# One home per chunk for the gathered rows of a recommendation tower, one semaphore per gathered slot, and the loops over chunks written out

## The reference

```
e = jnp.stack([tbl_0[ids[:, 0]], ..., tbl_25[ids[:, 25]]], axis=1)   # 512 x 26 x 64
x = layer_norm(dense_t @ Wd.T, gd, bd)                                # 512 x 128
y = layer_norm(jnp.einsum('bnd,ed->bne', e, Ws), gs, bs)              # 512 x 26 x 128
y = jnp.einsum('bne,pn->bep', y, Wsi)
y = jnp.swapaxes(layer_norm(y, gsi, bsi), 1, 2)                       # 512 x 32 x 128
T = jnp.concatenate([x[:, None, :], y], axis=1)
Z = jnp.einsum('bnd,bmd->bnm', T, T)                                  # 33 x 33 per sample
z = layer_norm(Z[:, TRIL_I, TRIL_J] @ Wl.T, gl, bl)                   # 512 x 512, 384 used
h = relu(concatenate([z, dense_t]) @ W_top1 + b_top1)
y = relu(h @ W_top2 + b_top2) @ W_top3
```

## Time and profile before

| what | value |
|---|---|
| time, median of 3 runs | 259.2 us (258.77 to 259.23) |
| profiled execution, span from first to last instruction | 258.3 us |
| PE busy | 183.6 us (71%) |
| DVE, ACT busy | 100.9 us (39%), 90.1 us (35%) |
| POOL busy, x104 gathers of 966 ns mean | 101.3 us (39%) |
| mean granted TensorE clock | 0.822 |

### The profile page before, as it was taken

The page is one execution under the profiler, slowest core; times in us unless marked ns, Lnnn a source line. Parts: engine busy times, 40 slices in busy tenths (PEclk is TensorE's granted clock), DMA queues, the critical chain, the costliest instruction groups (busy, mean ns, idle before and its releaser), DMA issues.

```text
span 258.3 us, 4239 instructions
## 1 busy us (share of the span) xinstructions
PE 183.6 (71%) x1616; PEld 117.3 (45%) x1616; DVE 100.9 (39%) x193; ACT 90.1 (35%) x221; POOL 101.3 (39%) x113
## 2 busy tenths in 40 slices
PE   1696913859295662948487569574849989999996
PEld 1343903516144252625264433443446466649476
DVE  2766003361078270526263401615254288623120
ACT  2442100710073340636034302523235276522333
POOL 4887772777405265445373720727250000000000
PEclk9999555695779595698777959859597999999999
DMA  6423235111100011015210100134110004123000
GB/s 171 150 67 111 56 107 173 28 27 25 20 1 19 15 21 22 10 20 129 41 23 10 33 10 0 22 94 68 21 25 0 0 0 116 27 86 53 3 0 0
DMA packets 19391, 11.67 MB, mean 45 GB/s; under 512 B 14256, under 2 KB 16816, under 8 KB 19376
## 3 DMA queue, kind: packets, MB, share of 16 engines
q1 hardware_dynamic: 16048, 8.05, 11.5%
q0 software_dynamic: 3328, 3.41, 6.9%
HBM read 9.29 MB, written 2.16 MB: 44 GB/s over the span
## 4 chain that ended last, share of the span: by engine, by line
PE 52%; issue 21%; another core or an unknown queue 13%; DVE 8%; ACT 4%; DMA 1%; SPq 0%; ACTq 0%; DVEq 0%
PE proj_ps L482 12%; PE dots_ps L473 8%; PE o_ps L501 6%; PE mix_ps L450 4%; PE quad_ps L461 4%; DVE var_p L786 2%; PE proj_ps L518 2%; PE turn_ps L501 2%; PE turn_ps L442 1%; PE proj_ps L396 1%; PE o_ps L505 1%; PE mix_ps L518 1%; PE o_ps L551 1%; PE dots_ps L551 1%
## 5 line engine op out<-in xcount | busy, mean ns | idle before, releaser
L373 POOL DMA_INDIRECT e_rows<-table_dram,rows_sb x104 | 100.5, 966 | 90.3 <-DVE e_unit L822 59.6
L473 PE MATMUL dots_ps<-feats 128*32 128x33 f32 x1024 | 27.0, 208 | 46.1 <-issue 45.9
L482 PE MATMUL proj_ps<-f_sb,proj_w 128*128 128x512 f32 x64 | 47.2, 878 | 5.7 <-issue 3.2
L473 PEld LDWEIGHTS dots_ps<-feats 128*32 128x32 f32 x1024 | 18.5, 117 | 55.8 <-issue 54.0
L786 DVE TENSOR_REDUCE var_p<-y_sq 128x16 f32<-128x512 f32 x32 | 21.4, 683 | 24.3 <-ACT y_sq L616 21.5
L818 DVE RECIPROCAL rstd_n<-std_n 128x8 f32<-128x8 f32 x16 | 3.2, 201 | 66.3 <-ACT std_n L636 61.5
L450 PE MATMUL mix_ps<-mixw_sb,e_unit 128*128 128x192 f32 (+4 forms) x128 | 21.7, 315 | 10.3 <-DVE e_unit L822 10.3
L616 ACT ACTIVATE y_sq<-proj_ps 128x512 f32<-128x512 f32 x32 | 18.7, 595 | 28.0 <-PE proj_ps L482 14.5
L482 PEld LDWEIGHTS proj_ps<-f_sb,proj_w 128*128 128x128 f32 x64 | 15.4, 266 | 22.8 <-issue 17.1
L450 PEld LDWEIGHTS mix_ps<-mixw_sb,e_unit 128*128 128x128 f32 x128 | 20.4, 201 | 11.0 <-DVE e_unit L822 10.9
L461 PEld LDWEIGHTS quad_ps<-gram,e_cols 128*128 128x128 f32 x104 | 18.5, 244 | 12.2 <-issue 12.1
(11 more groups left out here) (131 smaller groups left out, 179.2 us busy)
## 6 DMA issues: line engine op xcount, KB each, us to landing
z_dram<-z_mine SPq DMA_DIRECT2D x4, 512.0 KB
e_rows<-table_dram,rows_sb POOLq DMA_INDIRECT x104
w_sb<-w_dram SPq DMA_DIRECT2D x2, 512.0 KB, 4.7
wl_sb<-wl_dram SPq DMA_DIRECT2D x2, 512.0 KB
w_sb<-w_dram SPq DMA_DIRECT2D x1, 768.0 KB
z_pairs<-z_dram SPq DMA_DIRECT2D x12, 64.0 KB
dense_sb<-dense_t_dram SPq DMA_DIRECT2D x1, 512.0 KB
wl_sb<-wl_dram SPq DMA_DIRECT2D x1, 256.0 KB
```

The source lines that it names most:

```text
L373: pool.indirect_dma_start(out=e_rows[:, t, D * ab:D * (ab + 1)], out_offset=None, in_=table, in_offset=bass.IndirectOffsetOnAxis(ap=rows_s ...
L473: mm = pe.matmul(dots_ps[PR * k:PR * (k + 1), (PR + 1) * g:(PR + 1) * (g + 1)], f[:, 2:PR + 2], f[:, 0:PR + 1], start=True, stop=True)
L482: pe.matmul(proj_ps[:, ab, :], proj_w[:], f_sb[:, q % 2, ab, :], start=True, stop=True).then_inc(projected, 1)
```

## The change

`e_rows` gets a second index, the chunk, so each gathered row has a place of its own and POOL waits for nothing but the row numbers. There is one semaphore per slot (16 in place of 4), and the waits on it are for 32 times its number of tiles in every chunk. The helper `slots` runs all steps from a Python loop, so nothing is a hardware loop any more on PE, ACT, DVE or SP, and every wait compares with a constant. What is computed, its order on each engine and the sizes of all instructions are the same.

```
-        e_rows = sb("e_rows", [P, TILES, 2 * D])
+        e_rows = sb("e_rows", [P, CHUNKS, TILES, 2 * D])
...
-        gathered = [sem(f"gathered{q}") for q in range(QUARTERS)]
+        gathered = [[sem(f"gathered{chunk}_{q}") for q in range(QUARTERS)] for chunk in range(CHUNKS)]
...
-            peeled = -(-latest // QUARTERS) * QUARTERS
-            for s in range(peeled):
-                slot(s // QUARTERS, s % QUARTERS, s)
-            with eng.Fori(peeled // QUARTERS, CHUNKS) as chunk:
-                for q in range(QUARTERS):
-                    slot(chunk, q)
-            for s in range(SLOTS, SLOTS + latest):
+            for s in range(SLOTS + latest):
                 slot(s // QUARTERS, s % QUARTERS, s)
...
-            return with_last(lambda chunk: None if isinstance(chunk, int) else stage(chunk))
+            return with_last(lambda chunk: stage(chunk) if chunk < CHUNKS - 2 else None)
...
-            sp.wait_ge(gathered[0], 32 * tiles_of(0)[1])
+            sp.wait_ge(gathered[0][0], 32 * tiles_of(0)[1])
...
-            with sp.Fori(1, CHUNKS - 1) as chunk:
+            for chunk in range(1, CHUNKS - 1):
...
-                    wait(pool, unit_ready, QUARTERS * (chunk - 1) + q + 1)
...
-                                out=e_rows[:, t, D * ab:D * (ab + 1)], out_offset=None, in_=table,
+                                out=e_rows[:, chunk, t, D * ab:D * (ab + 1)], out_offset=None, in_=table,
...
-                            ).then_inc(gathered[q], 16)
+                            ).then_inc(gathered[chunk][q], 16)
...
-                pe.wait_ge(gathered[q], chunk * (32 * nt) + 32 * nt)
+                pe.wait_ge(gathered[chunk][q], 32 * nt)
...
-                    mm = pe.transpose(turn_ps[:, P * t:P * (t + 1)], e_rows[:, t0 + t, :], eye_sb)
+                    mm = pe.transpose(turn_ps[:, P * t:P * (t + 1)], e_rows[:, chunk, t0 + t, :], eye_sb)
```

More of the change, by code:

```diff
@@ L260, in tower, with slots, slot @@
         block = ctx.enter_context(nc.Block())
-        def slots(eng, stages, extra=()):
+        def slots(stages, extra=()):
             latest = max(late for late, _ in stages)
-            def slot(chunk, q, s=None):
+            def slot(chunk, q, s):
                 for late, stage in stages:
-                    if s is None or 0 <= s - late < SLOTS:
+                    if 0 <= s - late < SLOTS:
                         stage(chunk + (q - late) // QUARTERS, (q - late) % QUARTERS)
@@ L314, in _ @@
             sp.dma_start(pairs_sb[:], pairs).then_inc(pairs_in, 16)
-            sp.wait_ge(gathered[0], 32 * tiles_of(0)[1])
+            sp.wait_ge(gathered[0][0], 32 * tiles_of(0)[1])
             sp.dma_start(w1_sb[:, 0:KU, :], w1[:, 0:KU, :]).then_inc(w1_in, 16)
             for q in range(1, QUARTERS):
-                sp.wait_ge(gathered[q], 32 * tiles_of(q)[1])
+                sp.wait_ge(gathered[0][q], 32 * tiles_of(q)[1])
                 begin, end = (q - 1) * KZ // 3, q * KZ // 3
@@ L526, in top_1_early @@
                 top_1(0, 0, CHUNKS - 2)
-            slots(pe, [(3, project), (1, quad), (0, turn), (2, mix), (4, dots), (8, in_loop(turn_o)), (7, in_loop(linear))],
+            slots([(3, project), (1, quad), (0, turn), (2, mix), (4, dots), (8, in_loop(turn_o)), (7, in_loop(linear))],
                   extra=[(1, sum_x), (1, top_bl), (3, lambda: weigh_moments(0, 3)),
@@ L708, in save_o @@
                          o_turn_ps[:, 0:USED].rearrange("p (j s b) -> p j s b", s=1, b=P)).then_inc(o_saved, 1)
-            slots(act, [(8, in_loop(square_o)), (2, root_n), (3, square), (3, root_p), (8, in_loop(root_o)),
+            slots([(8, in_loop(square_o)), (2, root_n), (3, square), (3, root_p), (8, in_loop(root_o)),
                         (8, in_loop(scale_o)), (0, save_cols), (3, place_x), (2, save_f), (4, save_z), (8, in_loop(save_o)),
@@ L794, in variance_n @@
                 wait(dve, std_ready, s)
-                dve.wait_ge(gathered[q], chunk * (32 * nt) + 32 * nt)
+                dve.wait_ge(gathered[chunk][q], 32 * nt)
                 dve.tensor_tensor(e_prod[:, 0:2 * nt, :].rearrange("p a d -> p (a d)"), quad_ps[:, 0:P * nt],
-                                  e_rows[:, t0:t0 + nt, :].rearrange("p t d -> p (t d)"), ALU.mult).then_inc(prod_done, 1)
+                                  e_rows[:, chunk, t0:t0 + nt, :].rearrange("p t d -> p (t d)"), ALU.mult).then_inc(prod_done, 1)
                 dve.wait_ge(prod_done, s + 1)
@@ L822, in norm_n @@
                 dve.tensor_tensor(e_unit[:, t0:t0 + nt, :].rearrange("p t (a d) -> p (t a) d", d=D),
-                                  e_rows[:, t0:t0 + nt, :].rearrange("p t (a d) -> p (t a) d", d=D),
+                                  e_rows[:, chunk, t0:t0 + nt, :].rearrange("p t (a d) -> p (t a) d", d=D),
                                   rstd_n[:, 0:2 * nt].unsqueeze(2).to_broadcast([P, 2 * nt, D]),
@@ L867, in invert_o @@
                 dve.reciprocal(o_rstd[:], o_std[:]).then_inc(orstd_done, 1)
-            slots(dve, [(2, norm_n), (8, in_loop(variance_o)), (3, variance_p), (8, in_loop(invert_o)), (3, norm_p),
+            slots([(2, norm_n), (8, in_loop(variance_o)), (3, variance_p), (8, in_loop(invert_o)), (3, norm_p),
                         (1, variance_n)],
```

## The result

| what | before | changed |
|---|---|---|
| time, median of 4 runs | 259.0 us (258.0 to 259.2) | 282.4 us (281.3 to 282.9) |
| profiled span | 258.3 us | 281.1 us |
| PE busy | 183.6 us | 153.1 us |
| mean granted TensorE clock | 0.822 | 0.780 |

The ratio is 1.090, 95% interval 1.086 to 1.095. The change costs 23 us, and 282.4 lies outside the range of the prediction; of its cases "frozen", 275 us, comes nearest.

What follows compares the result with a forecast made beforehand. Gathers on POOL were taken to slow PE's completions. PE free at about 138 us and step 5 at 147 or 141, plus 72.0 and 46.3 us, gave spans of 265.3 and 259.3, forecast 262 us, range 246 to 271.

Steps and rivals of the forecast that it cites:

- frozen: Rival: PE's completions stand still while gathers run, step 5 starts at 156 us, time 275 us; chance 0.13 with nearly frozen.
- The bound: Gathers are almost never late; while they run, PE completes passes at a small rate, so POOL's pauses matter.
- first sign: ACT and DVE show "remote" waits of tens of us before 138 us, the first at L829, past 41.8.
- the release: PE is free 1.4 to 3.6 us after POOL's last gather at 135.7 us, so from about 138 us.
- The second: the rate: Beside gathers without a break PE completes 0.57 to 0.83 passes per us, 64 to 93 passes by 138 us.
- the low rate: 0.57 passes per us: PE at the end of step 3 when freed at 138 us, step 5 starting near 147.
- the high rate: 0.83 passes per us: 93 passes, PE in step 4 when freed at 138 us, step 5 starting at 141.
- the two spans: Predicted profiled spans of 265.3 us at 0.57 passes per us and 259.3 us at 0.83, middle 262.
- The short-batch rate: Rival: PE keeps 1.9 to 2.9 passes per us beside gathers, kernel gets faster, put at 247 us; chance 0.38.
- rival 2: PE keeps the short batches' rate of 1.9 to 2.9 passes per us beside gathers, 247 us; chance 0.38.

Runs made afterwards that it cites:

- set 4 pair: Changed kernel unedited, 282.1 us, and changed kernel with only POOL's 12 waits put back, 256.6 us, on a chip where before took 260.9 us.
- e16_half_rows: Changed kernel with gathers of 64 rows in place of 128, on a chip where before took 260.9 us: 287.9 us.
- e1: Changed kernel with POOL's wait put back, on a chip where before took 194.4 us: 192.1 us, ratio 0.990.
- e9: Changed kernel with POOL's wait put back, on a second chip where before took 194.2 us: 193.1 us, ratio 0.998.
- e15: Changed kernel with a 512-column memset on POOL before each gather, one gather each 1.78 us, where before took 260.9 us: 244.6 us.

## Why the prediction was wrong

**What held.** The bound and the sign of its mechanism: gathers are almost never late on a held chip, they slow PE's completions, and the change takes away the pauses. The set 4 pair puts 25.5 us on POOL's wait, more than the 21.2 us that the change lost in that set, and so nothing on the written-out loops and semaphores, as the prediction had it. Its first sign came true as well: L821, which is L829 of before, started at 71.15, past 41.8. That it got slower was forecast with a chance of 0.52 only. POOL's end, 135.7 predicted, is 136.03. After the release: steps 5 to 15 were to cost 72.0 us and took 73.25 (161.43 to 234.68); the rest from step 16, 46.3 predicted, took 46.4. `dots` of step 4 did come in one burst after the release (158.90), though none of them before it.

**The step that failed: the release.** "With 1.4 to 3.6 us for the release PE is free from about 138 us" took the lag after a batch for a constant. It grows with the batch. The rows had it: after the first 26 gathers the lag was 3.6 us, after 20 also 3.6, after the six of step 5 about 1.4, and I carried the values on as they were. Set against the number of gathers they are 0.14, 0.18 and 0.23 us each, which gives 14 to 24 us for 104; 14.85 were measured, and that the first batch comes so close is luck, since the three disagree. What does agree is the time from the start of a batch to its release: 1.46, 1.42 and 1.42 us per gather (the last from 78.99 to 87.5), and 1.415 in the new one. The step cost 12.9 us (150.88 against 138).

**The second: the rate.** "I take 0.57 to 0.83." From 71.15 to 118.68 PE completed 0.36 passes per us, and from 25.8 to the release 54 passes in 125 us (24 of `top_bl`, 17 of step 2, 13 of step 3), 0.43. The 8 passes in 14.1 us ended at the release itself, at which any number that PE had ready would have come through at once, so they were no low end; the 5 in 6.0 us were rows, and rows are not completions. So at the release ACT had results up to `turn` of step 3, while PE's rows stood at the end of step 3, waiting for ACT: the place that the low rate was to give at 138, reached only because the release was late. Step 5 started 10.5 us behind the release, where 9 had been reckoned from this place and 3 at the high rate: `f_sb` cost 1.3 us for 1.2, and step 4 cost 9.2 (152.22 to 161.43) for 7.2. Of the 18.8 us by which the middle of the two spans missed (281.1 less 262.3), 12.9 are the release, 3 the rate (9 less the middle, 6), 1.5 step 4, 1.25 the steps after and 0.1 the rest.

**The rivals.** The short-batch rate fell: no batch was short any more. "Frozen" had the state of PE at the release nearly right (in step 2 or 3) but the release at 138 too; with 150.9 in its place its 275 would be 288, so PE is not frozen, it crawls. That the measured time lies nearest to it is luck. `e16_half_rows`, which had its release at 150.11 with PE still in step 2, took just that, 287.9 us.

**The cost of a long batch, put together.** Before, at 150.9 us, PE was in step 10, with slow steps still ahead; after the change it was in step 3 and had steps of 5. Those made up for most, not for all: step 16 starts 22.6 us later (234.68 against 212.04), which is all but 0.2 us of the difference between the spans. While gathers come in batches with gaps, PE does a full step's rows in each gap, and the hold runs off while POOL waits for `e_unit` anyway. In one batch PE has no gap for 147 us.

**The rule weighed there.** The runs show both sides. On unheld chips, and on a held one with plain DMAs, `dots` take 0.77 us beside the transfers. So far the trace agrees with the Trainium skill, "SBUF — State Buffer", section "Who interferes with whom", that DMA never contends with a compute engine. On held chips the same gathers keep PE's results back, and there the measurement decides: by that rule the prediction had rival 2, 247 us, or better, and the change took 282.4.

**What stays open.** What a held chip is: I found nothing in the traces but the hold itself that tells the chips apart. Why the gather by index holds PE and a plain DMA does not, and why each TensorE instruction then waits 1.40 us over long stretches, nearly the figure of one gather's hold. One instruction let through per gather would give both, but that is argued from the numbers alone, and two things speak against it: with half the rows they part (1.39 us an instruction, 1.37 a gather), and beside the short batches of before PE's rows of `dots` came each 0.71 us, one to five at a time.

```profile
84.68 0.32 PE L473 MATMUL dots_ps<-feats 128*32 128x33 f32 x3 [0.52 <-issue]
85.39 0.21 PE L473 MATMUL dots_ps<-feats 128*32 128x33 f32 x1 [0.40 <-issue]
86.10 0.32 PE L473 MATMUL dots_ps<-feats 128*32 128x33 f32 x3 [0.49 <-issue]
```

The changed kernel was never run on an unheld chip. From e1 and e9, with 0.6 us of POOL's wait left, I would expect it within a few tenths of a per cent of them, an estimate. The spacing at 1.42 us was never run on a held one. Loops kept and the buffer enlarged alone wasn't tried. And no version was shown to be clearly faster than before on both kinds of chip: e15, the best with gathers by index on a held one, is the worst on the others.

## What to carry to other kernels

A wait can be worth its time: look at what the waiting engine does to the others once nothing stops it. When a lag follows a batch of work, hold it against batches of several sizes, and the time from the start of each batch to its release too, before taking it for a constant, and don't carry a lag or a rate from short batches into one four times as long. And run a kernel with many gathers by index on more than one chip before tuning it: here a change of chip was worth 65 us, more than any edit but those that took out the gathers by index.

## What the hardware showed that I had not expected

- The same kernel takes 194 us on some chips and 259 on others, each within 2% either way (256.6 and 192.1 for the kernel with the wait put back, traced on both), and what differs in the traces is that gathers by index from POOL hold back TensorE's completions: 1.42 us per gather of 128 rows, 1.37 per gather of 64.
- It outlasts its cause: 14.85 us without a gather and with the DMA engines 1% busy, after 104 of them.
- A plain DMA from POOL (0.53 us) or from SP leaves no hold on the same chip.
- PE's rows can stand 46 us ahead of the moment at which their result reaches another engine (`mix` at 72.20, ACT at 118.68). Where rows and releases differ, the releases are to be believed.
